# Eight more down products of each batch in three fp32r passes, with two buffers for the parts of the experts' values and four for the values

## The reference

```python
scores = sigmoid(x @ router_w.T)            # 64 experts, 8 groups, 4 groups kept, top 8 experts
coef = scores of the 8 chosen experts, normalised, times 2.5, else 0
h = silu(x @ Wg[e]) * (x @ Wu[e]) * coef[:, e]     # 64 experts, 64 columns each
moe_out = sum over e of h[e] @ Wd[e]
shared = silu(x @ SWg) * (x @ SWu) @ SWd           # one shared expert, 128 columns
x = layernorm(x + moe_out + shared)
```

## Time and profile before

| what | value |
|---|---|
| median of 3 runs (lowest, highest) | 1030.04 us (1029.47, 1031.43) |
| the profiled execution's own time | 1028.34 us |
| its span, first to last instruction | 1026.3 us |
| granted TensorE clock, mean | 0.985 |
| PE busy | 958.7 us (93%) |
| DVE busy | 810.6 us (79%) |
| POOL busy | 623.0 us (61%) |
| ACT busy | 463.4 us (45%) |

### The profile page before, as it was taken

The page is one execution under the profiler, slowest core; times in us unless marked ns, Lnnn a source line. Parts: engine busy times, 40 slices in busy tenths (PEclk is TensorE's granted clock), DMA queues, the critical chain, the costliest instruction groups (busy, mean ns, idle before and its releaser), DMA issues.

```text
span 1026.3 us, 16151 instructions
## 1 busy us (share of the span) xinstructions
PE 958.7 (93%) x5014; PEld 576.6 (56%) x5014; DVE 810.6 (79%) x2438; ACT 463.4 (45%) x882; POOL 623.0 (61%) x666
## 2 busy tenths in 40 slices
PE   5799989999999899999999999999999999988996
PEld 2344456665666556665566555665566556655553
DVE  5666767799978997799977997789977986587554
ACT  2344445445444445444444444454444445433332
POOL 2432227674776557675676657765676567766774
PEclk8699999999999999999999999999999999999999
DMA  8441053323633254323623244322633322322331
GB/s 296 133 148 59 27 169 128 116 83 101 199 106 116 87 164 134 116 79 99 206 98 115 95 141 148 128 74 80 215 91 118 103 94 90 97 87 90 102 112 63
DMA packets 63077, 120.79 MB, mean 118 GB/s; under 512 B 7056, under 2 KB 34576, under 8 KB 62608
## 3 DMA queue, kind: packets, MB, share of 16 engines
q1 hardware_dynamic: 62992, 119.76, 36.3%
HBM read 97.32 MB, written 22.02 MB: 116 GB/s over the span
## 4 chain that ended last, share of the span: by engine, by line
PE 59%; DVE 30%; issue 5%; DMA 2%; POOL 2%; ACT 1%; SPq 0%; POOLq 0%; DVEq 0%
PE acc L614 7%; DVE max_out L912 6%; PE sm L531 6%; DVE hid L985 5%; PE st L549 5%; PE pg L490 5%; PE ob L561 4%; PE pu L490 4%; DVE hid L976 4%; PE pg L492 4%; PE pg L491 4%; PE pu L492 4%; PE pu L491 4%; PE acc L486 3%; PE acc L604 2%
## 5 line engine op out<-in xcount | busy, mean ns | idle before, releaser
L728 POOL TENSOR_TENSOR hid<-hid,coef_b 128x512 f32<-128x512 f32 x255 | 329.8, 1293 | 193.0 <-DVE hid L985 155.9
L677 ACT ACTIVATE hid<-pg 128x512 f32<-128x512 f32 x264 | 157.8, 598 | 363.8 <-PE pg L492 363.2
L912 DVE CUSTOM_DVE_ANT_0 max_out<-sm,causal_sb 128x128 bf16<-128x128 f32 (+3 forms) x512 | 236.7, 483 | 97.0 <-PE sm L531 95.5
L976 DVE SCALAR_TENSOR_TENSOR hid<-hid,pg 128x512 f32<-128x512 f32 x264 | 180.1, 682 | 84.3 <-ACT hid L677 84.3
L732 POOL TENSOR_TENSOR hid_lo<-hid,hid_hi 128x512 fp32r<-128x512 f32 x127 | 163.5, 1287 | 76.0 <-ACT hid_hi L684 74.7
L649 ACT ACTIVATE probs<-st 128x512 f32<-128x512 f32 (+1 forms) x384 | 187.6, 526 | 34.5 <-PE st L549 33.0
L985 DVE TENSOR_TENSOR hid<-hid,pu 128x512 f32<-128x512 f32 x256 | 174.4, 681 | 9.3 <-PE pu L492 5.3
L490 PE MATMUL pg<-x_hi,wg_hi 128*128 128x512 f32 x256 | 144.1, 563 | 16.9 <-DVE hid L976 16.8
L531 PE MATMUL sm<-k_stack,q_stack 72*128 72x128 bf16 (+3 forms) x512 | 138.4, 311 | 13.5 <-DMA k_stack<-k_rows_dram 9.1
L714 POOL TENSOR_SCALAR_AFFINE_SELECT probs<-probs 128x256 f32<-128x256 f32 x256 | 102.3, 424 | 75.3 <-ACT probs L649 74.9
L490 PE MATMUL pu<-x_hi,wu_hi 128*128 128x512 f32 x256 | 125.1, 488 | 10.5 <-DVE hid L985 10.4
(11 more groups left out here) (134 smaller groups left out, 1271.4 us busy)
## 6 DMA issues: line engine op xcount, KB each, us to landing
coef_b<-coef_dram SPq DMA_DIRECT2D x128, 512.0 KB, 3.9
q_rows_dram<-qk_parts SPq DMA_DIRECT2D x24, 384.0 KB, 3.3
k_rows_dram<-qk_parts SPq DMA_DIRECT2D x24, 384.0 KB, 3.6
q_stack<-q_rows_dram SPq DMA_DIRECT2D x64, 144.0 KB
k_stack<-k_rows_dram SPq DMA_DIRECT2D x64, 144.0 KB
xT_sb<-in_xT SPq DMA_DIRECT2D x8, 256.0 KB, 3.9
y<-in_x SPq DMA_DIRECT2D x8, 256.0 KB, 4.5
out<-out_sb SPq DMA_DIRECT2D x8, 256.0 KB, 2.7
```

The costliest lines, as they stand in the source:

```text
L728: pool.tensor_tensor(hid[:, i % 3, :], hid[:, i % 3, :], coef_b[:, half % 2, j, :], ALU.mult)\
L912: last = dve.tensor_tensor_reduce(out=max_out[:, seg.nth(BANK_SM, task) % 2, col:col + wide], in0=sm_of(seg, task)[:, col:col + wide], in1 ...
L976: dve.scalar_tensor_tensor(hid[:, i % 3, :], hid[:, i % 3, :], 1.0, pg[:, :], ALU.add, ALU.mult).then_inc(a_done, 1)
```

## The change

`split_down` takes, besides the odd units, those with u % 4 == 2 (units 2, 6, ..., 30): eight in each batch, 64 in all. Their weights move from `wd_sb`, now half as wide, to `we_hi` and `we_lo`, which a tenth chunk fills in the prologue. `hid` gets four buffers (`slot`), `hid_hi` and `hid_lo` two each. `hi` and `lo` of the new units stand at u + 2.2 and u + 2.3, and `h` of all even units at u + 1.2 instead of u + 1.6. `for_dve` goes away: POOL does the last `lo` and `h` too.

```diff
-MOE_EVEN = {'u': 0.513, 'a': 0.25, 'b': 0.763, 'd': 2.813, 'h': 1.6}
+MOE_EVEN = {'u': 0.513, 'a': 0.25, 'b': 0.763, 'd': 2.813, 'h': 1.2, 'hi': 2.2, 'lo': 2.3}
 MOE_ODD = {'u': 0.65, 'a': 0.15, 'b': 0.658, 'd': 2.95, 'h': 0.9, 'hi': 1.9, 'lo': 2.0}
...
-WEIGHT_LOADS = (-5.881, -4.25, -0.25, 2.9, 5.15, 6.8, 8.95, 12.296, 15.45)
-WEIGHT_SPLITS = (-0.861, 2.046, 5.9, 6.7, 9.03, 9.15, 9.249, 15.9, 15.949)
+WEIGHT_LOADS = (-5.881, -4.25, -0.25, 2.9, 5.15, 6.8, 8.95, 12.296, 15.45, 17.5)
+WEIGHT_SPLITS = (-0.861, 2.046, 5.9, 6.7, 9.03, 9.15, 9.249, 15.9, 15.949, 19.0)
...
 def split_down(u):
-    return u % 2 == 1
+    return u % 2 == 1 or u % 4 == 2
...
-        wd_sb = sb("wd_sb", [P, PAIRS // 2 * D])
+        we_hi, we_lo = sb("we_hi", [P, PAIRS // 4 * D], F32R), sb("we_lo", [P, PAIRS // 4 * D], F32R)
+        wd_sb = sb("wd_sb", [P, PAIRS // 4 * D])
...
-        hid = sb("hid", [P, 3, S])
-        hid_hi, hid_lo = sb("hid_hi", [P, S], F32R), sb("hid_lo", [P, S], F32R)
+        hid = sb("hid", [P, HIDDEN, S])
+        hid_hi, hid_lo = sb("hid_hi", [P, 2, S], F32R), sb("hid_lo", [P, 2, S], F32R)
...
+        even = Wd[:, PAIRS // 2 * D:].rearrange("p (k two d) -> p k two d", two=2, d=D)
+        chunks.append((even[:, :, 0, :], we_hi[:, :], we_lo[:, :], coef_flat[:, 0:narrow], 3))
...
-        def for_dve(task):
-            return task in (("lo", B - 1, UNITS - 2), ("h", B - 1, UNITS - 1))
+        def slot(n, i):
+            return (n * UNITS + i) % HIDDEN
...
                         if split_down(i):
-                            w = slice(i // 2 * D, (i // 2 + 1) * D)
+                            half = seg.nth(("hi",), ("hi", n, i)) % 2
+                            if i % 2:
+                                w_hi, w_lo = (w[:, i // 2 * D:(i // 2 + 1) * D] for w in (wd_hi, wd_lo))
+                            else:
+                                w_hi, w_lo = (w[:, i // 4 * D:(i // 4 + 1) * D] for w in (we_hi, we_lo))
                             after(pe, seg, low_done, ("lo",), ("lo", n, i))
-                            pe.matmul(acc[:, :], wd_hi[:, w], hid_hi[:, :], start=first, stop=False)
-                            pe.matmul(acc[:, :], wd_hi[:, w], hid_lo[:, :], start=False, stop=False)
-                            pe.matmul(acc[:, :], wd_lo[:, w], hid_hi[:, :], start=False, stop=last)\
+                            pe.matmul(acc[:, :], w_hi, hid_hi[:, half, :], start=first, stop=False)
+                            pe.matmul(acc[:, :], w_hi, hid_lo[:, half, :], start=False, stop=False)
+                            pe.matmul(acc[:, :], w_lo, hid_hi[:, half, :], start=False, stop=last)\
                                 .then_inc(d_full, 1)
...
-                        before = (n, i - 3) if i >= 3 else (n - 1, UNITS + i - 3)
+                        before = (n, i - HIDDEN) if i >= HIDDEN else (n - 1, UNITS + i - HIDDEN)
...
                         before = seg.last(("hi",), task)
+                        before = before and seg.last(("hi",), before)
                         if before:
                             after(act, seg, d_full, ("d",), ("d", *before[1:]))
```

More of the change, by code:

```diff
@@ L31 @@
 RING = 8
+HIDDEN = 4
 STACK_PAIRS = NH // 2
@@ L34 @@
 SPLIT_BY_DVE = 3
-CHUNKS = 9
+CHUNKS = 10
 PARTS = 3
@@ L613, in tasks @@
                                 after(pe, seg, h_done, ("h",), ("h", n, i))
-                            pe.matmul(acc[:, :], w, hid[:, i % 3, :], start=first, stop=last).then_inc(d_full, 1)
+                            pe.matmul(acc[:, :], w, hid[:, slot(n, i), :], start=first, stop=last).then_inc(d_full, 1)
             pe.wait_ge(filler_done, 1)
@@ L676, in tasks @@
                             after(act, seg, d_full, ("d",), ("d", *before))
-                        act.activation(hid[:, i % 3, :], pg[:, :], ACT.Tanh, scale=0.5).then_inc(tanh_done, 1)
+                        act.activation(hid[:, slot(n, i), :], pg[:, :], ACT.Tanh, scale=0.5).then_inc(tanh_done, 1)
                     if kind == "hi":
@@ L681, in tasks @@
                         before = seg.last(("hi",), task)
+                        before = before and seg.last(("hi",), before)
                         if before:
                             after(act, seg, d_full, ("d",), ("d", *before[1:]))
-                        act.activation(hid_hi[:, :], hid[:, i % 3, :], ACT.Copy).then_inc(hidhi_done, 1)
+                        act.activation(hid_hi[:, seg.nth(("hi",), task) % 2, :], hid[:, slot(n, i), :], ACT.Copy).then_inc(hidhi_done, 1)
                     if kind == "fin":
@@ L720, in tasks @@
                             .then_inc(rstd_done, 1)
-                    if kind == "h" and not for_dve(task):
+                    if kind == "h":
                         after(pool, seg, b_done, ("b",), ("b", n, i))
@@ L727, in tasks @@
                             pool.wait_ge(c_in[half % 2], 16 * many)
-                        pool.tensor_tensor(hid[:, i % 3, :], hid[:, i % 3, :], coef_b[:, half % 2, j, :], ALU.mult)\
+                        pool.tensor_tensor(hid[:, slot(n, i), :], hid[:, slot(n, i), :], coef_b[:, half % 2, j, :], ALU.mult)\
                             .then_inc(h_done, 1)
-                    if kind == "lo" and not for_dve(task):
+                    if kind == "lo":
                         after(pool, seg, hidhi_done, ("hi",), ("hi", n, i))
-                        pool.tensor_tensor(hid_lo[:, :], hid[:, i % 3, :], hid_hi[:, :].bitcast(F32),
+                        pool.tensor_tensor(hid_lo[:, seg.nth(("hi",), ("hi", n, i)) % 2, :], hid[:, slot(n, i), :],
+                                           hid_hi[:, seg.nth(("hi",), ("hi", n, i)) % 2, :].bitcast(F32),
                                            ALU.subtract).then_inc(low_done, 1)
@@ L981, in tasks @@
                         if i == SHARED:
-                            ins = dve.scalar_tensor_tensor(hid[:, i % 3, :], hid[:, i % 3, :], 0.5, pu[:, :],
+                            ins = dve.scalar_tensor_tensor(hid[:, slot(n, i), :], hid[:, slot(n, i), :], 0.5, pu[:, :],
                                                            ALU.mult, ALU.mult)
                         else:
-                            ins = dve.tensor_tensor(hid[:, i % 3, :], hid[:, i % 3, :], pu[:, :], ALU.mult)
+                            ins = dve.tensor_tensor(hid[:, slot(n, i), :], hid[:, slot(n, i), :], pu[:, :], ALU.mult)
                         ins.then_inc(b_done, 1)
-                    if kind == "h" and for_dve(task):
-                        after(dve, seg, b_done, ("b",), ("b", n, i))
-                        half, j = divmod(i - 1, 2)
-                        many = sum(t[0] == "c" and (t[1], t[2]) <= (n, half) and t[2] % 2 == half % 2
-                                   for t in seg.tasks)
-                        if many and seg.nth(("c",), ("c", n, half)):
-                            dve.wait_ge(c_in[half % 2], 16 * many)
-                        dve.tensor_tensor(hid[:, i % 3, :], hid[:, i % 3, :], coef_b[:, half % 2, j, :], ALU.mult)\
-                            .then_inc(h_done, 1)
-                    if kind == "lo" and for_dve(task):
-                        after(dve, seg, hidhi_done, ("hi",), ("hi", n, i))
-                        dve.tensor_tensor(hid_lo[:, :], hid[:, i % 3, :], hid_hi[:, :].bitcast(F32),
-                                           ALU.subtract).then_inc(low_done, 1)
                     if kind == "finT":
```

14 lines of the change are left out of this document (8 added, 6 removed).

## The result

The change makes the kernel slower: 1124.22 us (median of 4 runs, 1119.81 to 1130.04) beside 1029.76 for the kernel before (4 runs, 1026.61 to 1031.43), a ratio of 1.0934 with a 95% interval of 1.0905 to 1.0962. The sign and the stops were forecast; the size was not: 94 us in place of 66, outside the range. Two parts of it had no term in the forecast's sum. The profiled execution took 1119.81 us.

A forecast was written before the change was run, and what follows sets the result against it. PE was taken to bound most of units 0 to 23, DVE units 24 and 28 on. Batches 0 to 6 (52.5), batch 7 with the end (12.6) and prologue (1.0) gave 66 us: 1096 us, range 1055 to 1112.

The forecast's parts named there:

- the chain and its stops: PE before down products of units 2, 6, ..., 30: unit 14's chain takes 3.46 us against 1.70 of work, so 1.75 idle.
- I cost it at nothing: Unit 22's product: 1.5 us late, but counted as nothing because DVE bounds there and PE waits for it a little later.
- in time: Unit 26's product: h of unit 27 ends at 578.98, so ready at 580.3 against 581.26, no stop.
- what is absorbed: Batches with attention: PE's present waits for DVE that a later PE won't have, 1.0 us a batch, bounds 0 and 4.
- Batch 7: No attention late in it: products 2.1 us late, net 1.6 per four units, 9.57 becomes 11.2; seven groups make 11.4.
- At the end: POOL instead of DVE does lo of 31 and h of 32, at 1.29 instead of 0.68: 1.2 us more.
- The prologue: One more chunk of 1024 columns, with hi and lo twice each: 1.0 us more, between 0 and 3.
- The stretch from unit 12: Sign in the profile after: these four units should take about 13.1 us instead of 11.55.
- The saving: Three passes instead of fp32 give back 0.16 us a product, 10.2 for 64 if PE bounds everywhere and nothing waits.
- The faster one: Rival: PE reaches d late enough because DVE sets the pace; 10.2 us saved at most, 1020; chance 0.05.
- Half absorbed: Rival: after a stall the other engines have caught up, shortening later waits; 1 to 5 us a batch, 1045 to 1070; chance 0.16.
- The block between POOL and DVE: Rival: two lo a batch hold up DVE by 1.1 us in units 24 to 32, 15 us, 1111; chance 0.12.

## Why the prediction was right and wrong

**Right: the chain and its stops.** Stops on PE before the new products of batch 3, measured after: units 2, 6, 10, 14, 18 and 30 have 1.59, 1.50, 1.30, 1.72, 0.97 and 2.00 us, forecast 1.7, 1.7, 1.4, 1.75, 1.0 and 1.9. The sum is 9.1 for a forecast of 9.5. Working forward from `g` of unit u + 2, instruction by instruction, gave each within 0.2. The run with the later product, in which they are gone with two thirds of the loss, shows that they are the cause.

**The steps that failed.** The sum had no term for the clock, which took 11 to 15 us, and it put the stops at units 22 and 26 at nothing, where the stretches with them grew by 0.73 and 0.52 us a batch even without the clock's part, some 9 us over seven batches. Together these are 20 to 24 of the 28 us that were missing.

**Unit 22: "I cost it at nothing".** The stop is 2.23 us, where I had 1.5. I overlooked `rstd`, which in the changed kernel runs between that `hi` and its `lo`:

```profile
600.25 0.62 ACT L695 ACTIVATE hid_hi<-hid 128x512 fp32r<-128x512 f32 x1
...
600.80 1.01 POOL L730 TENSOR_TENSOR rstd<-var_eps,half_power 128x4 f32<-128x4 f32 x1 [1.21 <-DVE var_eps L791]
...
601.78 2.51 POOL L743 TENSOR_TENSOR hid_lo<-hid,hid_hi 128x512 fp32r<-128x512 f32 x2
...
603.11 0.50 PE L614 MATMUL acc<-hid_hi,we_hi 128*128 128x512 f32 x1 [2.07 <-POOL hid_lo L743]
```

The rows before had it:

```profile
564.43 1.01 POOL L719 TENSOR_TENSOR rstd<-var_eps,half_power 128x4 f32<-128x4 f32 x1 [1.23 <-DVE var_eps L779]
564.51 0.59 PE L614 MATMUL acc<-hid,wd_sb 128*128 128x512 f32 x1
```

`lo` behind it and the step to PE make 564.43 + 1.01 + 1.29 + 0.06 = 566.79, 2.3 after the product's place. The cover that I named, PE's waits for DVE in units 24 to 27, did go, but in batch 3 it was 1.3 before `g` of unit 26 and 0.4 before a transpose. So the stretch grew by 0.73 in the run with fillers, and by 1.9 in the changed kernel, with an episode at 1.2 GHz behind the stop.

**Unit 26: "in time".** The stop is 1.34 us. I went from the tanh of unit 28 straight to `hi` of unit 26. On ACT a copy of the attention, `ev`, stands between the two and waits for PE's products into `ob`. After:

```profile
616.04 0.60 ACT L687 ACTIVATE hid<-pg 128x512 f32<-128x512 f32 x1 [1.79 <-PE pg L498]
...
618.36 0.60 ACT L663 ACTIVATE ev<-ob 128x512 f32<-128x512 f32 x1 [1.72 <-PE ob L567]
...
618.86 0.62 ACT L695 ACTIVATE hid_hi<-hid 128x512 fp32r<-128x512 f32 x1
...
619.56 1.26 POOL L743 TENSOR_TENSOR hid_lo<-hid,hid_hi 128x512 fp32r<-128x512 f32 x1 [2.23 <-ACT hid_hi L695]
...
620.87 0.50 PE L614 MATMUL acc<-hid_hi,we_hi 128*128 128x512 f32 x1 [1.18 <-POOL hid_lo L743]
```

and its place before:

```profile
580.09 0.60 ACT L653 ACTIVATE ev<-ob 128x512 f32<-128x512 f32 x1 [1.72 <-PE ob L561]
```

From there the forecast's own durations give 580.09 + 0.50 + 0.63 + 0.08 + 1.29 + 0.06 = 582.65 against 581.26, 1.4 late. The stop costs little all the same. DVE is busy for 16.52 of the 16.59 us of that stretch, and the 0.52 that it grew is there as well in the run in which no product waits; it is the block of the merge step.

**The clock, which the sum didn't have.** Every term took durations at 2.4 GHz. With the stops the granted clock fell more often, and filling them gave back 11 to 15 us. I had a mean clock of 0.985 before me and never asked what idle time does to it. It is the largest single miss.

**Off in size: what is absorbed.** I took 1.0 us per batch, with bounds 0 and 4. In batch 3 the sum closes: stops at all eight 12.65, savings -1.3, clock +1.2 (the stretch from unit 24 with and without fillers, 16.29 - 15.12), PE's waits for DVE before `g` and `u` -2.8 and the one before a transpose -0.4. That makes 9.4 for the measured +9.6. Forecast: 9.5 - 1.0 - 1.0 = 7.5. Batches 0 to 6 together grew by 73.5, forecast 52.5. Batch 6 has stops of 14.1 instead of 12.65; I had taken batch 3 for all seven.

**Batch 7** grew by 16.6 and the end by 2.6, together 19.2 for a forecast of 12.6. With fillers batch 7 grew by 11.4, the forecast's own number, though not by its steps: seven groups of 1.6 are 11.2, the stretches from unit 8 on are +1.84 each, and the first two are -0.4 and +0.8. The rest of the 16.6 is the clock (in turn +1.95 and +2.94 per stretch). The stop is 1.98 to 2.02, forecast 2.1. At the end, POOL in place of DVE is worth 0.9 of the forecast 1.2: the ends of three kernels that have it, and no new product in batch 7 that waits, are 0.9 longer, and that of the kernel that leaves it to DVE is unchanged.

**The prologue** is 1.0 shorter in this profile, where I had 1.0 longer. Profiles of the kernels above that have the same additional chunk range from -1.8 to +2.6, so this term can't be told.

**The stretch from unit 12** was to take 13.1 us as a sign. That added the stop of unit 14, whose product stands in the next stretch. The product in it is that of unit 10, and 11.55 + 1.4 - 0.16 is 12.8, as measured (12.79).

**The saving.** 0.16 per product is exact where PE bounds (11.55 to 11.38) and behind a stop. As a gain by itself it is 2 us over the run, not 10. The Trainium skill's four passes for true fp32 ("FP8 and Floating Point Precision", TensorE Precision Notes) would make it 0.23; the stretch from unit 12 disagrees with that, with its 0.17.

**The rivals.** The faster one assumed that PE comes late enough; the measured stops exclude it. "Half absorbed" named an effect that is there: some 3.2 us in batch 3, within its 1 to 5. But its price doesn't follow from that (7 to 35 us off 1096 are 1061 to 1089, not 1045 to 1070), and what the sum left out was larger. The block between POOL and DVE is there, at one place per batch. The Trainium skill ("SBUF — State Buffer", Who interferes with whom) calls the shared ports an exclusive lock that is held to the end of an instruction; 185 ns to 1125 ns for the same 32 columns, ending 0.05 us after POOL's instruction, agrees.

**What stays open.** The clock's price is known only to 11 to 15 us: two medians of four runs each scatter, and between the two profiled executions a few episodes fall in other places. The fillers may also lengthen a stop that is shorter than they are. PE's extra work time of about 22 us is larger than this price, since a slower PE waits less afterwards; that last step is argued, not shown.

## What to carry to other kernels

An additional step between a producer and a product is priced at the consumer's place in the order: add up the new chain from the last instruction that both share, and set it against the work the consumer has until then; busy shares of 45% and 61% said nothing about it. When a stop is put down as covered by another wait, measure how long that wait is. Read every instruction that stands in the helpers' queues in between: `rstd` on POOL and `ev` on ACT were the two that I passed over. And ask what stops do to the clock: here 106 us of them came with 11 to 15 us more through it, while a saving on an engine that isn't the bound in every stretch came to a fifth of its count.

## What the runs showed of the hardware

In this kernel the granted clock of TensorE fell behind stops of 1.6 to 2.2 us, but not behind each. In the changed kernel's profile the stop of 2.2 us for unit 22 is followed by an episode at 1.2 GHz in each of batches 0 to 5, and one of 2.8 us for the same unit in batch 6 by none. The 1.6 us for unit 2 is followed by one in batch 1 alone. The 2.0 us for unit 30 in batches 0 to 5 is followed by none, yet with one fp32 matmul behind the wait the same stop is followed by one in all six. So the length of a stop alone doesn't decide it; what does isn't shown.

An episode lengthened its stretch by 1.1 to 1.2 us: 1.17 in the stretch from unit 24, 1.23 in batch 1, 1.1 in batch 7. Five matmuls with zero weights ahead of the waits brought the episodes down from 16 to 4, and the whole was 11 to 15 us faster.

A DVE instruction of 32 columns takes 0.19 us or 1.14, by whether a POOL subtraction is running as it starts; leaving out that one POOL instruction gives the time back, 0.5 us of the stretch.
